# Layer 0 of a two-layer kernel: VectorE's share of each side job one tile later, gate steps, squares and normalising at other tiles

## The reference: what is computed

```
xn = layernorm(x)
q, k = (xn @ Wq.T), (xn @ Wk.T)            # 8 heads, each of 2 halves i of 16 channels
v = xn @ Wv.T                              # 8 heads of 32
att_i = softmax(q_i k_i / sqrt(16))        # 512 x 512 for each head and half
o = (att_0 - dw * att_1) @ v
s = ((o * rsqrt(mean(o*o) + eps) * norm_w) @ Wo.T + bo) * (1 - dw)
gate = top 2 of 8 of xn @ w_route.T, softmax over the two
g = silu(2 * sum(gate * (xn @ compress.T) @ routed))
x = x + s * g
```

## Time and profile before

| | us |
|---|---|
| median of 3 executions | 1274.58 |
| the three | 1273.21, 1274.58, 1279.83 |
| profiled execution, its own time | 1278.79 |
| its span | 1277.0 |

### The profile page before, as it was taken

One profiled execution on the slowest core, in us unless ns is written; L12 is line 12 of the kernel. 1 busy time (PEld: TensorE's weight loads), 2 busy tenths in 40 slices (PEclk: granted clock), 3 DMA queues, 4 the chain that ended last, 5 costly groups with the idle time before them and its releaser, 6 DMA issues. The chain is left out here.

```text
span 1277.0 us, 33870 instructions
## 1 busy us (share of the span) xinstructions
PE 1196.3 (94%) x13840; PEld 745.5 (58%) x13840; DVE 877.9 (69%) x1896; ACT 681.3 (53%) x1297; POOL 593.4 (46%) x611
## 2 busy tenths in 40 slices
PE   5889999999999999999976999999999999999997
PEld 4433444444443444443345787887878787787876
DVE  5866787777878777786635657576685757567665
ACT  2455667666666766665752544534454444445453
POOL 2056676676867667685732314223131413223131
PEclk9598999999999999999987999999999999999999
DMA  7634355453535545255031001010101001010100
GB/s 197 137 80 105 83 119 127 95 120 86 113 88 115 136 90 122 70 116 170 10 100 45 4 10 44 3 51 4 51 4 50 3 10 44 3 51 4 34 4 18
DMA packets 57994, 86.74 MB, mean 68 GB/s; under 512 B 8304, under 2 KB 38256, under 8 KB 57840
## 3 DMA queue, kind: packets, MB, share of 16 engines
q1 hardware_dynamic: 57840, 84.58, 27.3%
HBM read 50.40 MB, written 33.55 MB: 66 GB/s over the span
## 5 line engine op out<-in xcount | busy, mean ns | idle before, releaser
L979 DVE TENSOR_REDUCE negmax<-s_bank 128x1 f32<-128x512 f32 x512 | 331.7, 679 | 52.8 <-PE s_bank L670 52.8
L1143 POOL TENSOR_TENSOR room<-room 128x512 f32<-128x512 f32 x248 | 309.4, 1280 | 104.9 <-ACT room L820 104.9
L820 ACT ACTIVATE room<-t_bank 128x512 f32<-128x512 f32 x512 | 290.6, 599 | 87.6 <-PE t_bank L680 85.2
L670 PE MATMUL s_bank<-kst,qst 48*128 48x512 f32 x512 | 210.4, 484 | 21.0 <-DVE negmax L979 16.7
L680 PE MATMUL t_bank<-qst,kst 50*128 50x512 f32 x512 | 212.2, 476 | 9.7 <-ACT room L820 7.4
L680 PEld LDWEIGHTS t_bank<-qst,kst 50*128 50x128 f32 x512 | 84.1, 188 | 117.9 <-ACT room L820 65.2
L1857 POOL TENSOR_TENSOR win<-rt,apart 128x512 f32<-128x512 f32 x32 | 41.9, 1332 | 231.7 <-DVE rt L1687 231.7
L693 PE MATMUL a_bank<-room,v 128*32 128x512 f32 x1024 | 139.0, 615 | 0.0
L670 PEld LDWEIGHTS s_bank<-kst,qst 48*128 48x128 f32 x512 | 83.9, 193 | 48.6 <-DVE negmax L979 43.3
L1844 POOL TENSOR_TENSOR ex<-ex,rc 128x256 f32<-128x256 f32 x64 | 42.0, 655 | 141.8 <-DVE rc L1715 141.8
L1433 PE MATMUL pr<-xt_h,win_h 128*128 128x512 f32 x256 | 106.2, 415 | 0.5 <-issue 0.5
(11 more groups left out here) (247 smaller groups left out, 2266.2 us busy)
## 6 DMA issues: line engine op xcount, KB each, us to landing
park<-qk_h SPq DMA_DIRECT2D x128, 128.0 KB, 2.4
qst<-park SPq DMA_DIRECT2D x64, 192.0 KB, 3.8
kst<-park SPq DMA_DIRECT2D x64, 192.0 KB, 4.3
park<-qk_l SPq DMA_DIRECT2D x64, 128.0 KB, 2.4
room<-in_x SPq DMA_DIRECT2D x8, 512.0 KB, 5.7
xr<-in_x SPq DMA_DIRECT2D x8, 512.0 KB, 6.4
room<-x SPq DMA_DIRECT2D x8, 512.0 KB, 4.1
out<-so SPq DMA_DIRECT2D x32, 128.0 KB, 1.7
```

Of the source, the lines that this page charges most:

```text
L670: pe.matmul(s_bank[S_BANK[w]][:, :], qst[slot][rows, j, c * P:(c + 1) * P], kst[slot][rows, j, :], start=True, stop=True).then_inc(m.s_don ...
L820: act.activation(probs[:, c, j, :], t_bank[w % 2][:, :], ACT.Exp, scale=SCALE0).then_inc(m.exp_done, 1)
L979: dve.tensor_reduce(negmax[:, i_par, 2 * odd + j, c:c + 1], s_bank[S_BANK[w]][:, :], X, ALU.max, negate=True).then_inc(m.max_done, 1)
L1143: add = pool.tensor_tensor(sums[:, pair, h, :], probs[:, 2 * pair, h, :], probs[:, 2 * pair + 1, h, :], ALU.add)
```

## The change

All of it is in layer 0, in the tables of tiles, the order within a tile and the order in two queues.

- DVE's share of each side job runs in the tile after the job's slot, behind that tile's maximum (before: in the job's own tile). Gate steps come behind it, and a tile may have several.
- Statistics and their ends go from (2,11), (2,12), (2,14) to (1,9), (1,11), (1,12); the 18 gate steps to other tiles, the first at (0,12), the last at (2,6); the gate's exponential to (1,15).
- ACT's squares and normalising are done ahead of the side copy of their tile, at other tiles, two in one tile at some.
- On POOL `rstd_of` goes from behind the pair sum (2,1) to behind (1,1).
- On SP `place_max(i + 3, 3)` goes ahead of `fill_stacks(i + 5, 1)`, and `fill_stacks(i + 6, 2)` behind `place_max(i + 4, 0)`.

```diff
-STATS, NORM_ENDS, NORMS = ((2, 11), (2, 12)), (2, 14), ((3, 10), (3, 11), (3, 12), (3, 14))
-GATE = ((1, 7), (1, 8), (1, 11), (1, 12), (1, 13), (1, 14), (1, 15), (2, 3), (2, 4), (2, 7), (2, 8), (2, 10),
-        (2, 15), (3, 0), (3, 2), (3, 3), (3, 4), (3, 6))
-GATE_EXP = (2, 13)
-SQUARES = ((1, 11), (1, 12), (1, 14), (2, 0))
+STATS, NORM_ENDS, NORMS = ((1, 9), (1, 11)), (1, 12), ((3, 1), (3, 1), (3, 9), (3, 11))
+GATE = ((0, 12), (0, 13), (0, 14), (0, 15), (1, 4), (1, 4), (1, 5), (1, 5), (1, 6), (1, 8), (1, 13), (1, 14),
+        (2, 0), (2, 1), (2, 1), (2, 5), (2, 6), (2, 6))
+GATE_EXP = (1, 15)
+SQUARES = ((1, 9), (1, 11), (2, 1), (2, 1))
...
                     park_parts(i + 5)
+                place_max(i + 3, 3)
+                if not last:
                     fill_stacks(i + 5, 1)
-                place_max(i + 3, 3)
...
                     park_parts(i + 6)
-                    fill_stacks(i + 6, 2)
                 if b:
                     store_x1(b - 1, 2)
                 if not last:
                     place_max(i + 4, 0)
+                    fill_stacks(i + 6, 2)
                     park_parts(i + 7)
...
-                        if (hf, w) in NORMS and b < B - 2:
-                            normalise(b + 2, (NORMS.index((hf, w)),))
+                        if b < B - 2:
+                            for t in range(QT):
+                                if NORMS[t] == (hf, w):
+                                    normalise(b + 2, (t,))
+                        if not first:
+                            for t in range(QT):
+                                if SQUARES[t] == (hf, w):
+                                    side("SQ", b - 1, t)
...
-                        if not first and (hf, w) in SQUARES:
-                            side("SQ", b - 1, SQUARES.index((hf, w)))
...
-                        if (hf, w) in GATE:
-                            gate(b, GATE.index((hf, w)))
                         for (jh, jw), kind, i, k in jobs:
-                            if (jh, jw) == (hf, w):
+                            if UNITS * jh + jw + 1 == UNITS * hf + w:
                                 side(kind, i, k)
+                        for step in range(len(GATE)):
+                            if GATE[step] == (hf, w):
+                                gate(b, step)
...
                 add_pair(b, 1, 1)
+                if b < B - 2:
+                    rstd_of(b + 2)
                 if not first:
                     residual(b - 1, 0)
...
                 add_pair(b, 2, 1)
-                if b < B - 2:
-                    rstd_of(b + 2)
```

## The result

| | before | after |
|---|---|---|
| median, us | 1273.89 | 1297.22 |
| lowest and highest of 4 | 1271.53, 1279.83 | 1294.37, 1299.37 |
| profiled execution | 1278.79 | 1294.37 |
| its span | 1277.0 | 1292.5 |

The ratio is 1.0175, 95% interval 1.0133 to 1.0216: slower. The median lies above the forecast of 1286 and above the end of its range, 1293.

What follows compares the result with a forecast made beforehand. PE's own instruction list was taken to bound the kernel. Batches 1 to 5 gave 7.2, batch 6 2.5, batches 7 and 0 1.0 each: 11.7 us on 1278.79 makes 1290.5, less 4.2 for the median, 1286 (range 1273 to 1293).

Steps and rivals of the forecast that it cites:

- its term for batch 7: Batch 7: +1.0 us, from TA3 1.0 and a POOL pair-sum wait of 0.5 to 1, against about 0.8 won.
- the last line: From profiled execution to median: 1290.5 us became 1286, as before's median was 4.2 below its profiled execution.
- Part A: DVE's share of every side job one tile later: later drains of misc cost PE 5.0 us per batch.
- Rival 3: DVE drains: the maximum ahead fits into DVE's wait for ACT, all gains stay, 26 us less, 1249; chance 0.12.
- Part B: Gate steps and statistics moved, place_max ahead of fills: maxima come earlier, 2.7 us per batch gained with Part A's 0.40.
- Part C: ACT's squares and normalising ahead of its side copies: 1.4 us per batch gained, 0.85 of it from ZT to PROJ5.
- The collision of gate step 2: Tile (0,14): the step waits about 1.0 us for POOL's second pair sum, TA1 comes later; +1.45 per batch in all.
- rival 1: Gate step 2 gets in before POOL's pair sum: +0.9 us per batch, 1283; chance 0.18.
- Gate steps inside `rstd_of`: Steps 16 and 17 during POOL's power operation: not held up, so the sum takes nothing for them.
- rival 4: POOL holds DVE up whatever its instruction: M to WF1 0.45 us longer in six batches, 1289; chance 0.05.
- Batches 0 and 6: Batch 6: +2.5 us, with 1.05 less to win. Batch 0: +1.0, as M jobs cost 1.8 and about 0.8 returns.
- rival 5: Batch 0 or 7: longer waits bring one more 1.2 GHz stretch, some 3 to 4 us, 1290; chance 0.03.

Runs made afterwards that it cites:

- e10: The changed kernel once more, unedited: 1298.87 us, 1.0195 of the kernel before.
- e4: The changed kernel with DVE's share of the M jobs alone back in its own tile: 1279.59 us, 1.0023 of the kernel before.
- e2: The kernel before with only DVE's share of every side job moved one tile later: 1321.41 us, 1.036 of the kernel before.
- e1: The changed kernel with DVE's share of every side job back in its own tile: 1290.05 us, 1.0120 of the kernel before.
- e5: As e1, with the gate loop in front of the side jobs and gate steps moved to other tiles: 1270.72 us, 0.9958 of the kernel before.
- e8: The changed kernel with the edits of e5 and e6 together: 1266.77 us, 0.9922 of the kernel before.
- e6: The changed kernel with only fill_stacks(i + 6) put back ahead of place_max(i + 4) on SP: 1294.05 us, 1.0135 of the kernel before.
- e3: The changed kernel with both moves in SP's queue undone: 1296.53 us, 1.0169 of the kernel before.
- e7: The kernel before with only ACT's squares and normalising moved ahead of its side copies: median 1275.93 us.
- e9: e8 with DVE's share of WF and the last three PROJ one tile later, gate steps away from POOL's sums: 1257.32 us, 0.9867 of the kernel before.

## Why the prediction was wrong

The sign was right and the size was not: 1286 against 1297.2. Two steps failed: the sum for layer 0, above all its term for batch 7, and the last line, which carried the sum over to the median.

**The sum.** It gave 11.7 us more in layer 0; 18.6 were measured (18.1 in e10), 6.9 more than said. Batch 7 alone is 6.6 of that (7.6 for 1.0; 3.7 by e10), and batch 0 is 0.6 (3.4 by e10). The whole profiled execution looks nearer, 1294.4 for 1290.5, only because layer 1, with the same code, took 3.1 less in it.

**The median.** The last line took 4.2 off the sum, the distance of before's profiled execution (1278.79) from its median. But the changed kernel's profiled execution is not above its median, it is 2.9 below, and e10's is level with its own (1298.76, 1298.87). Without this step the same sum gives 1290.5. Executions of one kernel can lie 5 to 9 us apart (1294.37 and 1299.37 after, 1271.42 and 1280.21 before), and e10 shows where they differ: in batches 0 and 7, in stretches at 1.2 GHz and in layer 1. The changed kernel falls into more such stretches: the mean clock of its eight executions, e10's with them, is 0.959 to 0.964, and that of the 38 of before timed beside the experiments is 0.963 to 0.973. How much of the 23 us between the medians this makes is not shown.

**Part A, 5.0 per batch: right.** M to the next job 1.70 or 1.71 (said 1.70), TA2 to TA3 2.50 (2.49), XT0 to V, TA0 to TA1 and TA1 to TA2 2.50, PROJ4 to ZT 3.50. e4 measured its greatest term alone as 2.9, e2 the whole in the same places as 5.8, with 0.8 of slow gate steps in it. The argument "there is no slack to give", from the earlier trace rows, held in every place. Rival 3, the faster one, fell with it.

**Part B: right.** WF2 to PROJ6 is 4.82 (said 4.83), WF0 to M 4.01 (4.02), WF1 to WF2 3.82, TA3 to M 3.21 (3.14). These two pieces in PE's timeline after:

```profile
337.14 1.13 PE L659 MATMUL misc<-wo,ot 128*128 128x256 f32 x4
...
341.96 0.50 PE L608 MATMUL misc<-xt_h,wqk_h 128*128 128x512 f32 x1
```

They answer to the earlier trace rows, 5.95 apart there.

**Part C: right for the steady batch.** ZT (317.08) to PROJ5 (323.08) is 6.00, forecast 5.93. V(0,9) to TD is 3.47, PROJ7 to V 3.92 for 4.24.

**The collision of gate step 2: did not happen.** That was rival 1, given 0.18. DVE's and POOL's timelines after:

```profile
298.92 0.55 DVE L1003 RECIPROCAL rec<-misc 128x64 f32<-128x64 f32 x1
...
299.39 0.13 DVE L1043 TENSOR_TENSOR gt<-gt,rank 128x32 f32<-128x32 f32 x1
```

```profile
299.30 5.03 POOL L1149 TENSOR_TENSOR room<-room 128x512 f32<-128x512 f32 x4 [3.51 <-ACT room L821]
```

The places were forecast to 0.03 us (2.37 and 2.28 behind TD, said 2.34 and 2.28), and POOL's record does begin first, by 0.09. The step took 0.13 all the same, and TA0 to TA1 is 2.50. What failed is the reading that whoever's record starts first wins, by a margin of a tenth. The collision itself is real: the same step 0.02 to 0.04 behind the same sum took 1.28 to 1.31 (e1, e5, e8). Why it got in at 0.09 is open. Without it the period was +0.9 by my sum and is +1.15: the remainder is small differences in places I had at whole gains (TA3 to M 0.07, OT0 to OT1 2.40 for 2.34, two of 0.05 to 0.08). That batches 1 to 5 give 7.4 together where 7.2 was said is luck: 5 x 0.55 for a collision that did not come, and in its place 5 x 0.25 and one slow stretch of 1.6. In batch 6 the collision was counted too.

**Gate steps inside `rstd_of`: right.** POOL's power operation and steps 16 and 17, after, from the timelines of both engines:

```profile
330.94 1.04 POOL L1137 TENSOR_TENSOR rstd<-veps,mhalf 128x4 f32<-128x4 f32 x1
...
330.99 0.18 DVE L1066 TENSOR_TENSOR gt<-gt,gs 128x32 f32<-128x32 f32 x1
331.21 0.19 DVE L1069 TENSOR_TENSOR gt<-gt 128x32 f32<-128x32 f32 x1
```

Both ran at full speed inside it, as the row of before said; in the twelve traces 60 gate steps of two inputs begin inside a power operation of layer 0's `rstd_of`, and each took 0.17 to 0.20. The Trainium skill (page "SBUF — State Buffer", section "SBUF: two separate sides") has the shared port pair locked for the whole of an instruction; by it rival 4 would have come. The traces agree for POOL's adds of 128 x 512 (1.30 us in e5) and of 128 x 1024 (e1's 2.37 us) and not for this operation.

**Batches 0 and 6: near.** Batch 6 +2.35, said 2.5. Batch 0 +1.6, said 1.0, and +4.4 in e10, with a mean clock of 0.82 and 0.78 for 0.83 before (rival 5 in part); how much of it the jobs make was not taken apart.

**Batch 7, "1.0": this step failed.** It is 7.6 (4.7 in e10). I had written that `fill_stacks(i + 6)` behind `place_max(i + 4)`, and `park_parts(i + 7)` with the fill after it, slip 2 us "with some 20 tiles in hand: nothing". For their own reader that is true, in every batch, though the slip is 3.2 us in batch 7: the last fill is issued 4.8 behind T(0,0), 1.6 in e6. But a queue has other passengers: in batch 7 the six weight loads and then `place_max` of the next half stand behind them, and its reader, T(1,0), had no tiles in hand at all; PE was already waiting 1.72 us for it. "The first costs vanish behind a DMA wait that is there already" took that wait as a fixed time on the clock, where it moves with what is in front of it. e3 and e6 undo the move and get 6.6 us back (3.8 against e10's batch 7). T(1,0) comes 3.2 earlier in e6, and the rest is clock and what followed. No run of the seven with the fill ahead shows the loss, and all five with it behind do. The POOL wait, "0.5 to 1", was right in size: WF0 to M 5.96 for 4.89 with the clock up (e3, e6, e7, e10), and 6.24 here with part of it at 1.2 GHz.

What stays open: why e4 and e2 meet the slow stretches so much more often than the changed kernel with the same wait in the same place, why gate step 2 was not held up at 0.09 us, and how the clock's part of the difference between the medians divides over the batches.

## What to carry to other kernels

Before you move work within an in-order queue, look not only at who reads that work but at everything behind it, in the first and the last iteration too, where the queue holds other things; a wait that is there already is not cover if it is caused by the same queue. A drain that the next job waits for belongs as early as its input allows, and other work goes behind it only where the engine that waits has something else to do: the same change costs 5 us per batch at the jobs that another follows closely, and gives about 0.7 at the WF and PROJ jobs of e9, where the gate steps moved too. And a sum on one profiled execution can't be carried over to a median by its distance from that median: the distance is that execution's own.

## What the runs showed of the hardware

- A wait of 1.17 us of PE at TA3 was followed by 3.4 us at the 1.2 GHz level in some ordinary batches (1 to 5) and not in others: in one of five after, none in e10, two each in e3 and e6, three in e2, four in e4, so in 12 of 30. In the 30 of before, e1, e5, e7, e8 and e9, which don't have the wait, it never was, and their mean clock is 1.00. One stretch costs 1.4 to 1.6 us there (74.6 and 73.2 in e4; 77.7 and 76.1 after), so such a wait can cost more than twice its length.
- A DVE operation with two SBUF inputs that began 0.09 us behind the recorded start of a POOL add was not held up (299.39), one 0.23 behind was the earlier trace rows, the same step as the first 0.02 behind was (1.30, e5), and one 0.04 behind waited for all 2.37 us of `add_maps` (e1). The recorded starts don't tell who is first when they are a tenth apart.
- POOL's power operation on 128 x 4, 1.04 us long, held up none of the 60 two-input gate steps that began inside it (0.17 to 0.20 us each, twelve traces).
- Rows of maxima issued right behind six large weight loads on the same queue reached T(1,0) 8.7 us later (issued at 600.55, read at 609.24). T(1,0) follows the issue of the first of these loads by 12.6 to 13.3 us in the eleven traces in which it waits for the rows, wherever in the batch they are issued.
